# Block of two mixture-of-experts feed-forwards around an attention, one core: copies ahead of exponentials, score waits by bank, second loop's routing spread over three batches

## The reference, cut to what matters

```python
x = L0_attn_x                                    # (8, 1024, 128)
x = x + 0.5 * ffn(_layernorm(x))                 # first feed-forward loop
x = x + attn(_layernorm(x))
x = x + 0.5 * ffn(_layernorm(x))                 # second feed-forward loop

def attn(x):                                     # causal, one head of width 128
    Q, K, V = x @ Qw, x @ Kw, x @ Vw
    scores = Q @ K.T / sqrt(128) + mask
    return softmax(scores) @ V

def ffn(x):                                      # 16 experts of width 64, one shared of width 128
    scores = sigmoid(x @ Wg.T)
    idx, w = route(scores, bias_corr)            # 2 of 4 groups, then 4 of 16 experts; w normalised, times 2.5
    hid = relu(x @ W1.T) ** 2                    # all experts
    return sum_e w_e * (hid_e @ W2_e.T) + relu(x @ Ws1.T) ** 2 @ Ws2.T
```

## Time and profile before

| | |
|---|---|
| median of 3 runs | 753.97 us (751.87 to 755.33) |
| profiled execution | 754.41 us, span 752.5 us |
| busy: PE, DVE, ACT, POOL | 659.0, 594.8, 547.7, 537.5 us (88, 79, 73, 71%) |
| mean granted TensorE clock | 0.939 |
| chain that ended last | PE 36%, DVE 11%, issue 7%, ACT 4%, DMA 4%, POOL 3% |
| ACT exponential waits for DVE's maximum | 92.8 us over 64 |

### The profile page before, as it was taken

One profiled execution on the slowest core, in us unless ns is written; L12 is line 12 of the kernel. 1 busy time (PEld: TensorE's weight loads), 2 busy tenths in 40 slices (PEclk: granted clock), 3 DMA queues, 4 the chain that ended last, 5 costly groups with the idle time before them and its releaser, 6 DMA issues.

```text
span 752.5 us, 15290 instructions
## 1 busy us (share of the span) xinstructions
PE 659.0 (88%) x3395; PEld 511.5 (68%) x3395; DVE 594.8 (79%) x2650; ACT 547.7 (73%) x1138; POOL 537.5 (71%) x427
## 2 busy tenths in 40 slices
PE   4789999999999956777777777838999999999997
PEld 4567777777777745666566665736777777777775
DVE  5988988898989858567476695877888998998863
ACT  3588998988989656565565575434989889889885
POOL 3388899989889746454464463443889989989885
PEclk9999999999999988888788998788999999999999
DMA  9766857756766414454454443386286886787683
GB/s 249 165 138 146 167 119 162 160 131 151 161 140 140 88 22 78 80 109 64 80 95 78 82 95 72 70 168 146 63 169 146 176 186 144 169 183 156 153 181 89
DMA packets 129306, 97.31 MB, mean 129 GB/s; under 512 B 80992, under 2 KB 94960, under 8 KB 129264
## 3 DMA queue, kind: packets, MB, share of 16 engines
q1 hardware_dynamic: 127056, 96.24, 61.5%
q10 hardware_dynamic: 2208, 0.59, 0.4%
HBM read 72.70 MB, written 5.24 MB: 104 GB/s over the span
## 4 chain that ended last, share of the span: by engine, by line
PE 36%; DVE 11%; issue 7%; ACT 4%; DMA 4%; POOL 3%; SPq 0%; POOLq 0%; DVEq 0%; ACTq 0%
PE psum L1294 9%; PE psum L1296 8%; PE psum L1295 8%; DVE raw_max L1170 3%; DMA wb<-scratch 3%; PE psum L1528 2%; DVE zn L1188 1%; PE psum L1516 1%; PE psum L1517 1%; PE psum L1518 1%; PE psum L1367 1%; DMA scratch<-wT 1%; PE psum L1476 1%; POOL a_rstd L408 1%; POOL shared L513 1%
## 5 line engine op out<-in xcount | busy, mean ns | idle before, releaser
L425 POOL TENSOR_TENSOR shared_r<-shared,shared_r 128x512 fp32r<-128x512 f32 x256 | 326.5, 1296 | 64.8 <-ACT shared L610 62.5
L1041 DVE SCALAR_TENSOR_TENSOR s_sb<-psum,wb 128x512 f32<-128x512 f32 x256 | 175.5, 688 | 47.6 <-PE psum L1296 21.7
L609 ACT ACTIVATE shared_r<-s_sb 128x512 fp32r<-128x512 f32 x256 | 160.0, 625 | 46.7 <-DVE s_sb L1041 44.5
L610 ACT ACTIVATE shared<-s_sb 128x512 f32<-128x512 f32 x288 | 177.7, 619 | 17.7 <-DVE s_sb L1041 17.7
L513 POOL TENSOR_TENSOR shared<-s_sb,shared 128x128 f16<-128x128 f32 (+3 forms) x64 | 82.0, 1286 | 84.0 <-ACT shared L540 84.0
L1294 PE MATMUL psum<-x_hi,w_hi 128*128 128x512 f32 x288 | 127.9, 444 | 0.7 <-DVE s_sb L1041 0.7
L1294 PE MATMUL psum<-shared_r,w_hi 128*128 128x512 f32 x256 | 114.9, 449 | 0.4 <-POOL shared_r L425 0.4
L1295 PE MATMUL psum<-x_lo,w_hi 128*128 128x512 f32 x288 | 114.9, 399 | 0.0
L718 ACT ACTIVATE s_sb<-psum,nmax 128x128 f32<-128x128 f32 (+3 forms) x64 | 47.3, 739 | 92.8 <-DVE nmax L1173 91.5
L1296 PE MATMUL psum<-x_hi,w_lo 128*128 128x512 f32 x288 | 114.4, 397 | 0.0
L1295 PE MATMUL psum<-shared_r,w_hi 128*128 128x512 f32 x256 | 101.5, 396 | 0.0
(11 more groups left out here) (196 smaller groups left out, 1416.3 us busy)
## 6 DMA issues: line engine op xcount, KB each, us to landing
wb<-scratch SPq DMA_DIRECT2D x128, 512.0 KB, 8.4
out<-x_sb SPq DMA_DIRECT2D x16, 256.0 KB, 9.8
x_sb<-in_L_attn_x SPq DMA_DIRECT2D x4, 256.0 KB, 6.3
scratch<-wT SPq DMA_DIRECT2D x32, 32.0 KB, 1.9
w_raw<-in_L_ffn_W ACTq DMA_DIRECT2D x1, 512.0 KB, 5.9
w_raw<-in_L_ffn_W SPq DMA_DIRECT2D x1, 512.0 KB, 6.7
w_raw<-shared SPq DMA_TRANSPOSE x32, 2.8
wb<-shared SPq DMA_TRANSPOSE x32, 3.9
```

The lines of the kernel that those rows point to most:

```text
L425: nc.gpsimd.tensor_tensor(g_lo[:, j % RING, :], g_f[:, j % RING, :], g_hi[:, j % RING, :].bitcast(F32), ALU.subtract).then_inc(F.glo_done, 1)
L609: nc.scalar.activation(g_hi[:, j % RING, :], s_sb[:, j % RING, :], ACT.Square)
L610: nc.scalar.activation(g_f[:, j % RING, :], s_sb[:, j % RING, :], ACT.Square).then_inc(F.sq_done, 1)
L1041: ins = nc.vector.scalar_tensor_tensor(s_, h_, 0.0, wb[:, u, c, :], ALU.max, ALU.mult)
```

## The change

- ACT, attention: the copies `uT_copy`, `z_hi_copy` and `q_hi_copy` of a step come before `exp` and `prob_hi` of that step, not after; from batch 1 on `z_hi_copy` is called at t = 1 and 2 rather than 0 and 1, and `q_hi_copy` stays at 3 and 4. `z16_hi` stays behind.
- PE, `score`: at t = 4 it waits, in batches 1 to 5, for the low half of z (bank 1 read) instead of the low half of q half 0; in batch 6 still for q. At t = 5 it waits for q half 1 as before.
- Batch 1's statistics (`stats(1)`, `mean(1)`, its root on POOL) move from batch 0 into the last turn of the first loop (k = 10, 11, 13; POOL at step 14), batch 0's fp16 tokens (`z16_hi`) to k = 14, 15; batch 1's `normalise` from t = 2, 3 to t = 0, 1, its transposes from t = 3, 4 to 2, 3, its products from 5, 6 to 4, 5.
- `start_ffn` runs from k = -8 (batch 5) to 16. Group 0 has its statistics at k = -5, transposes at -2, routing at 0 to 5, weights' transpose at 6; group 1 routing at 5 to 12, transpose at 13; group 2 routing at 14 to 17. The call with k = 17 goes away on PE and ACT.
- SP: `keep(0)` is issued behind the transpose of tile 6 of batch 6, `spread(0, 0)` behind that of tile 7, with a wait until `mix` of batch 5 is complete; both stood behind the transpose of tile 4 of batch 7.
- DVE waits for `prob_lo` of the last two tiles before gates 0 and 2 of the second loop.

```diff
@@ SP @@
-                            if b == B - 1 and t == HQ:
+                            if b == B - 2 and t == QT - 2:
                                 keep(0)
+                            if b == B - 2 and t == QT - 1:
+                                sp.wait_ge(AT.mix_done, 4 * (B - 2))
                                 spread(0, 0)
@@ POOL @@
-                    if (b, t) == (B - 3, QT - 1):
+                    if (b, t) == (B - 3, 3):
                         inv(0)
-                    if (b, t) == (B - 2, 1):
+                    if (b, t) == (B - 2, 0):
                         inv(1)
+                    if (b, t) == (B - 2, 3):
+                        norm_root(0)
...
-                            if last and F is FF[0] and j == 4:
-                                attention_inv(0)
+                            if last and F is FF[0] and j in (4, 14):
+                                attention_inv((j - 4) // 10)
@@ ACT @@
-                            exp(b, t, u)
-                            prob_hi(b, t)
...
                             if t == 1 and b > 0:
                                 uT_copy(b - 1, 0)
                             if t == 6 and b > 0:
                                 uT_copy(b - 1, 1)
                             if b + 1 < B:
-                                z_at, z16_at, q_at = ((0, 1), (2, 3), (3, 4)) if b > 0 else ((3, 4), (4, 5), (5, 6))
+                                z_at, z16_at, q_at = ((1, 2), (2, 3), (3, 4)) if b > 0 else ((3, 4), (3, 4), (5, 6))
...
+                            exp(b, t, u)
+                            prob_hi(b, t)
...
-                            if b >= B - UN:
-                                start_ffn((b - (B - UN)) * QT + t)
+                            if b >= B - 3:
+                                start_ffn((b - (B - 2)) * QT + t)
@@ DVE @@
-                        if k == (0, 2, 8, 14, 16 if phase == 1 else 18)[n]:
+                        if k == ((-5, 0, 8, 13, 17) if phase == 1 else (0, 2, 8, 14, 18))[n]:
...
-                        if n < PREP and k == (1, 3, 9, 15)[n]:
+                        if n < PREP and k == (-3, 2, 10, 15)[n]:
                             second_half(n)
...
+                    for n, slots in ((0, {0: (0, 1), 1: (2, 3), 2: (4, 5, 6), 3: (7, 8), 5: (9,)}),
+                                     (1, {5: (0,), 6: (1, 2), 7: (3,), 8: (4, 5), 9: (6,), 10: (7, 8), 12: (9,)}),
+                                     (2, {14: (0, 1), 15: (2, 3), 16: (4, 5), 17: (6,)})) if phase == 1 else (
...
+                    if k in (10, 11):
+                        stats(1, k - 10)
+                    if k == 13:
+                        mean(1)
...
+                        if c % 2 == 0:
+                            v.wait_ge(A.plo_done, QT * B - 1 + c // 2)
                         lead_ffn(c)
@@ PE @@
-                        if k == (2, 4, 10, 17)[n]:
+                        if k == (-2, 3, 11, 16)[n]:
...
-                    if t in (HQ, HQ + 1) and 0 < b < B - 1:
-                        pe.wait_ge(A.qlo_done, 2 * b + 2 + t - HQ + 1)
+                    if t == HQ and 0 < b < B - 2:
+                        pe.wait_ge(A.zlo_done, 2 * b + 3)
+                    if t == HQ and b == B - 2:
+                        pe.wait_ge(A.qlo_done, 2 * b + 3)
+                    if t == HQ + 1 and 0 < b < B - 1:
+                        pe.wait_ge(A.qlo_done, 2 * b + 4)
```

88 lines of the change are left out of this document (38 added, 50 removed).

## The result

| | before | after |
|---|---|---|
| median (lowest to highest) | 754.62 us (751.87 to 755.33, 4 runs) | 710.26 us (709.84 to 712.78, 4 runs) |
| ratio, 95% interval | | 0.943 [0.939, 0.946] |
| span of the profiled execution | 752.5 us | 708.7 us |
| busy PE, DVE, ACT, POOL | 659.0, 594.8, 547.7, 537.5 | 643.1, 597.6, 547.0, 537.6 us |
| mean granted TensorE clock | 0.939 | 0.976 |

The kernel is 44 us faster: 710.26, where 704 were forecast with 691 to 729 around it. DVE, ACT and POOL do the same work in less time. Only PE's busy time fell, by 16 us, and not for fewer instructions (3395 in both profiles): where the gaps are shorter its clock was more often at the higher of its two levels, 2.4 GHz (batch 3: granted clock 0.79 before, 1.00 now).

The account below looks back on a forecast made before the run. A chain through several engines, none of them full, was taken to bound a steady attention batch; the seven parts sum to -50.7 us from the profiled 754.4, giving 703.7, rounded to 704, range 691 to 729.

Parts of the forecast that it names:

- Part 1: Batches 1 to 4: sooner scores at tile 4 and sooner q copies save 4.8 us a batch, 19.2 in all.
- Part 3: Batch 6: tile 5 sooner, faster clock, logits moved away and no wait before `values` save 7.0 us together.
- Part 2: Batch 5: the same 4.8 us less 1.9 for group 0's statistics and normalisation, so 2.9 saved.
- Part 4: Batch 7: five fewer routing parts at 0.57 us each and a shorter PE wait for group 2's tokens save 4.0.
- The load ahead of batch 7's first transposes: SP queue: landing may stretch to 11.3 us, but the first reader comes 12 us into batch 7; cost zero, worst 9.0.
- Part 5: Batch 0: statistics, mean and root moved to the first loop save 5.5 us, the moved fp16 subtraction 1.5; together 7.0.
- Part 6: Seam behind batch 7: earlier load and transposes, and routing gone from between the gates, start `values` 13.0 us sooner.
- Part 7: Attention batches: denser GpSimd work slows VectorE's normalising by 0.4 us a batch, giving 2.4 back over six batches.
- Tile 5 keeps its wait: Rival, chance 0.20: in attention, q half 1 stays late and only tile 4's 2.05 us wait is won; 717 us.
- The lock takes it: Rival, chance 0.15: the first normalisation of six batches takes 4.85 us, not 2.05; 721 us, or 738 with both.
- Earlier batches pay on: Rival, chance 0.08: mixes already free at a batch's start bring 1.5 us more in seven batches; 694 us.
- Transposes are late: Rival, chance 0.04: transposes land late before `mix` of tiles 4 and 5, 9.04 us in each of seven batches; 767 us.

Follow-up runs that it names:

- s5: The kernel before with the changed score waits and only the two q copies ahead of their exponentials, from batch 1 on; 722.89 us.
- s3: The kernel before with the changed score waits and the uT, z and q copies ahead of the exponentials, from batch 1 on; 720.27 us.
- the repeat: The changed kernel measured once more, without any edit; 710.52 us.
- a3: The changed kernel with the second loop's statistics of group 0 and their root one step later in batch 5, at t = 4; 709.01 us.
- s4: The changed kernel with the second loop's start (statistics, transposes, logits, routing, weights' store and load) put back to the places of the kernel before; 713.49 us.
- a2: The changed kernel with the 2 MB load in two halves, the second behind the transpose of tile 3 of batch 7; 708.46 us.
- a1: The changed kernel with the 2 MB load behind the transpose of tile 3 of batch 7 instead of tile 7 of batch 6; 713.16 us.

## Why the prediction was right, and where its terms were not

- **Part 1, batches 1 to 4: right in mechanism, too small.** -19.2 was -25.4, or 6.4 a batch. Its two waits are worth 5.5 (s5, forecast 4.8) and the uT and z copies add 1.2 (s3). That 6.4 is less than the sum of the two is batch 4's, which took 20.9 in s3 and 22.4 in the changed kernel (see the last section). The 1.2 go with the wait ahead of `values`. Part 3 counted it for batch 6 (1.5); part 1 didn't count it for batches 1 to 4. The "uncounted second gain" that part 1 names is another one, mixes that are free when a batch starts, and no run takes it apart.
- **Part 2, batch 5: right in number, by luck.** -2.9 forecast, -1.9 in the first profile and -3.0 in the repeat, but two errors cancel: the attention edits bring 6.7 to 6.9, not 4.8, and the second loop's work in this batch costs 3.7, not 1.9. a3 shows 1.4 of it to be the place of the statistics.
- **Part 3, batch 6: the step that failed.** "Together 7.0" was 0.7. The gain was looked for behind tile 4, and it is there: from tile 4's maximum to the next batch it is 17.0 before (451.70 to 468.68) and 12.0 after, 5.0 of the 7.0. What was left out is what the change adds ahead of it. Part 4 counts the parts that leave batch 7; part 3 never counted the parts that enter batch 6, where 4 became 14, nine of them ahead of tile 4's maximum. From the batch's first maximum to tile 4's it is 14.15 before and 18.3 after, and s4, with the routing at its old place, has 13.9. Seven parts of group 0 stand ahead of q half 0's subtraction, for which TensorE waits. In the changed kernel's trace they take 6.9 us of VectorE (406.33 to 408.32, 409.44 to 411.07 and 413.03 to 416.25), 0.98 each and not part 4's 0.57. Against that, 2.7 of group 0's statistics and normalisation left this stretch and 0.7 of group 1's entered it; the subtraction runs 15.2 us into the batch where s4 has it at 10.6. Even at 0.57 the seven would have been 4.0. The row was at hand; the question "what is added here" was not asked.
- **Part 4, batch 7: 4.0 forecast, +0.8 measured.** Its mechanism is there, at about half: s4 to a2, 25.1 to 22.8, 2.3. In the changed kernel the load's wait covers it.
- **The load ahead of batch 7's first transposes: failed.** "Their first reader is ScalarE's fp16 copy of tile 4, some 12 us into the batch, so I take zero." The reader and the stretched landing (11.3, 11.2 measured) were right. The place of the reader was right too: it would have come at 447.2, some 14 us into the batch, and waited 5.67. What was left out is when the transpose is issued. SP issues tile 0's at 441.63, behind the load and 8.1 us into the batch, and it lands 11.2 later, at 452.8. The prediction set a landing of 11.3 against a reader at 12, as if the issue stood at the batch's start; 8.1 + 11.2 is 19.3. In a2, behind half the load, the issue is 6.8 into the batch and the landing 7.4. Net cost 3.1 to 3.4 (a1, a2).
- **Part 5, batch 0: right,** 7.0 against 6.1, or 5.8 in a3.
- **Part 6, seam: right,** 13.0 against 11.4 for the move alone (s4 to after). The other 1.8 come with the attention edits (s4 against the kernel before). Of them, 0.2 are a later start of the mix of tiles 4 and 5, 13.6 us behind the last maximum instead of 13.4. 1.3 lie between that mix and the first gate: the matmuls there run at the lower level of the clock until `values` (eight take 1.50 us, before 1.05). Why the clock rose later isn't shown.
- **Part 7, VectorE against GpSimd: size wrong, place right.** The 56 normalisations take 29.3 us instead of 28.7, so +0.6, not +2.4; see the last section.
- **The rivals.** "Tile 5 keeps its wait": out (0.96 left); its sum takes 2.3 a batch where its text has 2.05. "The lock takes it": out as priced. "Earlier batches pay on": a further gain of that size came, 1.2 a batch, but with the wait ahead of `values`, not shown to be the mixes that it names. "Transposes are late" as a rule in every batch: out; it came once, at the load, which the text had called the only thing that ever made such a landing. The total came within 6.3 us by luck: the gain left out in part 1 (6.2) offset half of what failed in parts 3 and 4 (11.1).

## What to carry to other kernels

When work is moved, make two sums for every stage that it leaves and enters, and for each instruction added ask which later wait it stands ahead of: here one part less ahead of a subtraction made TensorE's wait for it 0.57 shorter, and two parts moved behind it brought nothing. In-order copies that other engines wait for belong ahead of work that only waits itself; that alone was 26 of 44 us. Here a large load in a queue of small transfers delayed all four behind it, so count from the issue and not from the landing alone, cut such a load, and put the pieces where their followers have the most slack.
